# POOL waits for each two transfers by index to land before it issues the next two

## What is computed

```
x = ln(x + attention(x))          # 16 heads of 128, causal
x = ln(x + experts0(x))           # 32 experts 96 wide, top 6 by sigmoid, one shared expert of 192
x = ln(x + ssm(x))                # Mamba-2 style mixing: in_proj, conv of 4 taps, scan, gate, out_proj
x = ln(x + experts1(x))           # 16 experts 176 wide, in 4 groups, top 4, one shared expert of 352
```

## Time and profile before

| | us |
|---|---|
| median of 3 runs | 1851.53 |
| lowest, highest | 1841.31, 1858.38 |
| the profiled execution's own time | 1850.39 |
| its span, first to last instruction | 1848.6 |
| busy PE, DVE, ACT, POOL | 1493.5, 995.6, 751.7, 448.7 |
| DMA: moved by index, by SP's transfers | 41.96 MB, 288.31 MB |

### The profile page before, as it was taken

The page is one execution under the profiler, slowest core; times in us unless marked ns, Lnnn a source line. Parts: engine busy times, 40 slices in busy tenths (PEclk is TensorE's granted clock), DMA queues, the critical chain, the costliest instruction groups (busy, mean ns, idle before and its releaser), DMA issues.

```text
span 1848.6 us, 30360 instructions
## 1 busy us (share of the span) xinstructions
PE 1493.5 (81%) x9344; PEld 1240.5 (67%) x9344; DVE 995.6 (54%) x3299; ACT 751.7 (41%) x2326; POOL 448.7 (24%) x422
## 2 busy tenths in 40 slices
PE   7999999999997342688856888984689998798992
PEld 6988988988986342577745666773456667566661
DVE  5777777777777320161114757542486764154345
ACT  5555655655653100244423436430243633233420
POOL 1000000001000747100033420815342080222133
PEclk9999999999998655799987999995799999899996
DMA  8472461551600214089976755853155586799922
GB/s 301 159 263 68 193 254 39 229 219 50 253 1 1 94 56 156 29 276 313 315 250 185 237 167 162 266 156 122 53 180 180 166 260 193 240 297 309 321 90 74
DMA packets 173078, 331.71 MB, mean 179 GB/s; under 512 B 17280, under 2 KB 85888, under 8 KB 171680
## 3 DMA queue, kind: packets, MB, share of 16 engines
q1 hardware_dynamic: 157600, 288.31, 47.2%
q0 software_dynamic: 15360, 41.96, 6.8%
HBM read 196.41 MB, written 133.27 MB: 178 GB/s over the span
## 4 chain that ended last, share of the span: by engine, by line
PE 49%; DVE 17%; another core or an unknown queue 10%; issue 9%; ACT 7%; DMA 5%; POOL 2%; SPq 1%; DVEq 0%; ACTq 0%; POOLq 0%
PE psum L426 40%; DMA l_os<-b_out 4%; PE psum L1633 2%; DVE x L1142 2%; PE psum L1455 2%; ACT p_sb L766 1%; DVE s_sb L1171 1%; PE psum L1604 1%; PE psum L1466 1%; DVE conv L1256 1%; DVE stats L976 1%; DVE x L990 1%; ACT p_sb L764 1%; ACT kT_hi L742 1%
## 5 line engine op out<-in xcount | busy, mean ns | idle before, releaser
L426 PE MATMUL psum<-xbT,bw 128*96 128x128 f32 (+1 forms) x2392 | 325.7, 285 | 13.0 <-issue 6.8
L426 PEld LDWEIGHTS psum<-xbT,bw 128*96 128x96 f32 (+1 forms) x2392 | 298.5, 186 | 18.9 <-issue 11.2
L666 POOL DMA_INDIRECT og<-l_os,l_back_of x160 | 160.4, 1003 | 510.0 <-DMA l_os<-b_out 282.8
L426 PE MATMUL psum<-bw,b_act 96*128 96x256 f32 (+2 forms) x692 | 222.6, 413 | 72.3 <-ACT b_out L839 27.1
L1159 DVE TENSOR_TENSOR b_act<-psum,b_gated 96x128 f32<-96x128 f32 x190 | 53.9, 285 | 334.9 <-ACT b_gated L826 265.4
L650 POOL DMA_INDIRECT xs<-x,row_of x160 | 165.6, 1035 | 221.0 <-DVE row_of L1062 176.3
L426 PEld LDWEIGHTS psum<-bw,b_act 96*128 96x128 f32 (+2 forms) x692 | 107.8, 196 | 115.5 <-issue 74.8
L426 PE MATMUL psum<-l_shared_w,b_act 128*128 128x256 f32 (+1 forms) x192 | 71.4, 470 | 135.2 <-issue 71.6
L1154 DVE TENSOR_TENSOR b_act<-psum,b_gated 128x128 f32<-128x128 f32 x126 | 36.6, 290 | 254.4 <-ACT b_gated L823 198.2
L614 POOL TENSOR_TENSOR aw_lo<-aw_raw,aw_hi 128x512 fp32r<-128x512 f32 x32 | 41.2, 1291 | 484.7 <-ACT aw_hi L732 484.7
L839 ACT ACTIVATE b_out<-psum 128x256 f32<-128x256 f32 x252 | 96.7, 384 | 139.4 <-PE psum L426 83.8
(11 more groups left out here) (217 smaller groups left out, 3726.4 us busy)
## 6 DMA issues: line engine op xcount, KB each, us to landing
xs<-zeros SPq DMA_DIRECT2D x42, 1792.0 KB, 17.4
bw<-l_w SPq DMA_DIRECT2D x94, 640.0 KB
bw<-l_w SPq DMA_DIRECT2D x158, 320.0 KB
xb<-xs SPq DMA_DIRECT2D x252, 128.0 KB
l_os<-b_out SPq DMA_DIRECT2D x124, 256.0 KB
decay_all<-decay_dram SPq DMA_DIRECT2D x32, 384.0 KB
aw_raw<-attn_w SPq DMA_DIRECT2D x8, 1024.0 KB, 6.9
xs<-x,row_of POOLq DMA_INDIRECT x160
```

Of the source, the lines that this page charges most:

```text
L426: last = nc.tensor.matmul(out_ap, w, m, start=start and n == 0, stop=stop and n == len(pairs) - 1, **kw)
L666: pool.indirect_dma_start(og[:, i % MIX_RING, k, :], None, os[f["layer"]][t // HALF_TILES], bass.IndirectOffsetOnAxis(ap=back_of[f["layer" ...
```

## The change

A helper `transfer` issues every transfer by index. It keeps the semaphore values that the transfers issued since the last wait will bring. When two have been issued, it waits for both values before it issues a third; where both add to one semaphore, one wait on the later value stands for the two. The counts that a transfer's semaphore will have reached are worked out from what earlier transfers added to it (`earlier`), as constants. The order of all instructions, the transfers themselves and their semaphores stay as they are; nothing waits at the end of a run of transfers, only before the next transfer, so multiplications that follow a pair are not held up by it.

```diff
@@ -639,16 +639,31 @@
                 group(g)
             low_part(GROUPS - 1, 3)
 
+
+            latest = {}
+
+            def transfer(*args, done, value):
+
+                if latest.get("count") == 2:
+                    for semaphore, v in latest["values"]:
+                        pool.wait_ge(semaphore, v)
+                    latest.clear()
+                pool.indirect_dma_start(*args).then_inc(done, 16)
+                latest["values"] = [(s, v) for s, v in latest.get("values", ()) if s is not done] + [(done, value)]
+                latest["count"] = latest.get("count", 0) + 1
+
             def scatter(f, q, part=None):
 
                 if part in (None, 0):
                     if f["layer"] == 0 and q == 0:
                         pool.wait_ge(xs_zeroed, 16 * ZEROED * (GROUPS - 1))
                     pool.wait_ge(placed, QUADS * f["layer"] + q + 1)
+                earlier = f["layer"] * QUAD * L0["top"]
                 rows = [(t, k) for t in range(QUAD * q, QUAD * (q + 1)) for k in range(f["top"])]
-                for t, k in rows if part is None else rows[part:part + 1]:
-                    pool.indirect_dma_start(xs[q // 2], bass.IndirectOffsetOnAxis(ap=row_of[:, t, k:k + 1], axis=0), x[:, t, :], None) \
-                        .then_inc(scattered[q], 16)
+                for r, (t, k) in enumerate(rows):
+                    if part in (None, r):
+                        transfer(xs[q // 2], bass.IndirectOffsetOnAxis(ap=row_of[:, t, k:k + 1], axis=0), x[:, t, :], None,
+                                 done=scattered[q], value=16 * (earlier + r + 1))
 
             def all_stored(f, h):
 
@@ -662,9 +677,11 @@
                 i = f["layer"] * TILES + t
                 if ks[0] == 0:
                     wait(pool, combined, i - MIX_RING + 1)
+                earlier = sum(LAYERS[j // TILES]["top"] for j in range(i % MIX_RING, i, MIX_RING))
                 for k in ks:
-                    pool.indirect_dma_start(og[:, i % MIX_RING, k, :], None, os[f["layer"]][t // HALF_TILES],
-                                            bass.IndirectOffsetOnAxis(ap=back_of[f["layer"]][:, t, k:k + 1], axis=0)).then_inc(og_loaded[i % MIX_RING], 16)
+                    transfer(og[:, i % MIX_RING, k, :], None, os[f["layer"]][t // HALF_TILES],
+                             bass.IndirectOffsetOnAxis(ap=back_of[f["layer"]][:, t, k:k + 1], axis=0),
+                             done=og_loaded[i % MIX_RING], value=16 * (earlier + k + 1))
 
             def ssm_constants():
                 pool.wait_ge(o_added, LAST_OUT)
```

## The result

The changed kernel takes 1878.78 us (median of 4 runs, 1874.00 to 1889.06), the kernel before 1854.95 us beside it (4 runs, 1841.31 to 1871.95). The ratio is 1.0148, with a 95% interval of 1.0108 to 1.0189: slower by 1.5%, where the forecast said 1818 us and faster. The profiled execution of the changed kernel took 1877.07 us, its span is 1875.3 us.

A forecast was written before the change was run, and what follows sets the result against it. POOL's transfers, issued every 1.27 us but each occupying something shared for about 1.40, bound 603 to 754 us; elsewhere PE, except where POOL paces. -82 + 14 + 35 = -33 from 1850.4 gives 1818 us, eight-in-ten range 1765 to 1868.

The forecast's parts named there:

- Part (a): 603 to 787 us: stalls beside POOL's first scatter vanish, -94, less +12 drag by the pairs: -82 us.
- cover of 9 us: Near 700 us: scatter lets unit 32 start at 696, units arrive at 705; gone if a pair costs 0.4 us more.
- Part (b): 787 to 936 us: the other 24 scatter pairs now run beside the routed units on busy DMA: +14 us.
- Part (c): Stretches POOL paces, from 942 us to the end: waits cost more than cured stalls give back, together +35 us.
- gathers at 942: From 942.77 us: 24 gathers take 58 us instead of 46 and combining DVE waits for them: +8 us (0 to 12).
- run from 1237: From 1237 us: 14 pairs take 54 us against 35, but a 22 us stall goes: +4 us (-10 to 19).
- scatter at 1567: From 1567 us: 17 us of stalls go, but the scatter ends 9 us later: -9 us (-17 to 0).
- end: End of the kernel: eight gathers take 16.6 us against 8.9 + 2.9, all on the path: +5 us.
- The price of a pair: Time for two transfers with their wait: 3.6 us for quiet scatters, 4.2 for quiet gathers, 6.2 beside busy DMA.
- Stalls half cured: 603 to 776 us: signals are still held up, a unit takes 3.6 us, drag 50 instead of 12: 1856 us; 17%.
- waits turn out cheap: Whole kernel: quieter DMA makes all pairs cost 3.6 to 4.2 us and later costs mostly vanish: about 1758 us; 8%.
- Only waits: Mainly 603 to 776 us: stalls come from transfers' presence, not their rate, so pacing only adds waits: 1927 us; 14%.

The follow-up runs named there:

- free sittings: Sittings, each on one chip, in which the unchanged kernel before ran at 1705.56, 1708.08 and 1706.33 us.
- held: Sittings in which the unchanged kernel before ran at 1859.01 and 1855.64 us, as in the case itself (1854.95 us).
- experiment 85: Not a run's number: 85 us by experiment, between pairs in layer 0's scatters alone (1787.34 us) and pairs everywhere (1876.08 us), each against the kernel before.
- last sitting: Changed kernel rerun unedited beside the kernel before at its quicker level (1706.33 us): 1879.56 us, ratio 1.0998.
- the first and the third sitting: Two sets of follow-up runs with partial pacing or slower feeding; the unchanged kernel before took 1705.56 us in one, 1855.64 us in the other.
- Fours in the scatters: POOL waits after four transfers in the scatters of both layers, gathers unpaced, against the kernel before at 1855.64 us: 1781.03 us, ratio 0.9606.

## Why the prediction was wrong, point by point

**What bounds the kernel** was read rightly for the traced condition: the stalls from 603 to 754 us come with POOL's transfers, and slower feeding takes them away wholly or for the most part, in four different ways. That they might be a condition of the sitting and not of the kernel was nowhere considered; the runs shown (1841 to 1858) gave no hint of the level at 1706, and that profiled time and median agreed couldn't rule it out, since all were taken at one level. The 1.40 us a transfer is a figure of that level: in the free sittings the same feed of one in 1.27 us holds up nobody in 603 to 664 us. It is not the reason for the miss, as the case was measured held, but it is the reason why the gain there can't be counted on.

**Part (a), -82 forecast, -74.9 measured** at unit 32. Two errors met. Unit 10 came at 649 instead of 660: no drag by pairs (in the changed kernel PE is as busy from 603.70 to 664.50 as in the free kernel before, 49.13 and 49.07 us). But the cover of 9 us under the scatter's first half was not there. A pair in the quiet takes 3.93 us, not 3.6, since POOL goes on 1.70 us after its second issue has ended, and some are longer beside loads; the half's rows were complete near 704 instead of 690, and SP and PE waited (53.4 and 29.3 us). The forecast had named 0.4 us a pair as the point from which that cover is gone.

**Part (b), +14 forecast, +7.2 measured** (unit 32 to 111). With (a) that is -67.7, where the forecast had -68: partly luck, as (a) was 7 us off one way and (b) 7 the other. Pairs in layer 0's scatters alone gave -68.3 for the whole kernel.

**Part (c) is the step that failed: +35 forecast, +94.4 measured**, and by experiment 85 (from -68.3 with layer 0's scatters alone to +17.1 with all). Term by term, from the table above:

| stretch | forecast | measured |
|---|---|---|
| gathers at 942 (unit 111 to 123) | +8 | +15.2 |
| gathers at 1033, scatters at 1157 (to 172) | +9 +8 | +18.5 |
| run from 1237 (to 199) | +4 | +24.2 |
| gathers at 1357, scatters at 1481 (to 244) | +6 +8 | +14.0 |
| scatter at 1567 (to 252) | -9 | +6.5 |
| gathers at 1637 (to 299) | -4 | +6.8 |
| end | +5 | +9.2 |

The four mixed terms, transfers among multiplications, were right within 2 us. The largest miss is the run from 1237. The forecast priced the 28 transfers that ran there without a pause, 14 pairs. But behind them stood 24 more gathers of the same half, issued in two more runs after pauses of 13.24 and 6.21 us in which POOL waited for a combine. In the kernel before that was slack, and all 52 transfers took 84 us (1237.32 to 1321.80). With gathers at 4.1 to 4.8 us a pair the slack is used up, and the 52 become one chain of 114 us (1211.89 to 1326.07) on which DVE, and PE behind it, wait. At the forecast's own prices the 26 pairs would be 8 x 3.6 + 18 x 4.2 = 104 us, so 20 of the 30 us more come from the count of the transfers and 10 from the price. It is the same from 942 on, where the forecast priced 24 gathers and 36 became one chain of 89 us (875.53 to 964.60), and at the end: from 1790.36 to 1861.26 POOL issues 32 gathers in pairs, one chain again, where the forecast priced the last eight. The second miss is 1567: the forecast took off 17 us of stalls as a gain and counted 9 us for the later scatter, but its end stands before SP's load of the half's first rows (SP waits 21.6 us there, PE 16.9), and it was later by the growing delay of a pair beside loads, 5.3 to 6.4 us for the first three.

**The price of a pair** was the smaller error: 3.6 and 4.2 us in the quiet were taken for landing plus 0.3 us. Measured are 3.93 and 4.1 to 4.8. Beside loads the forecast had 6.2, and the second scatter's 24 pairs took 154.6 us, 6.4 each.

**The rivals.** "Stalls half cured" and "waits turn out cheap" are both out: nothing of the stalls is left in 603 to 754 us, and (c) cost more, not less. "Only waits" (1927 us) was right in its sign and wrong in its mechanism: it had the stalls stay. Yet its sentence from the Trainium skill ("DMA: Bandwidth & Descriptors", Rules for kernel authors: issue early, wait late) names what cost: by the last sitting, obeying it is worth 173 us where nothing stalls. The other sentence of the Trainium skill ("SBUF — State Buffer", SBUF: two separate sides), by which DMA and the compute engines cannot slow each other there, agrees with the free trace (PE busy 49.07 us beside 48 scatters), and the held one doesn't contradict it: there the engines' instructions are no longer, only further apart. That pacing would then cure nothing, as the prediction concluded, doesn't follow: the stalls have another cause and pacing cures them all the same.

**What stays open.** What puts a sitting at one level or the other was not found. It isn't the program, and it isn't a chip's number as recorded: the first and the third sitting bear the same one, free and held. Nor was it found what the transfers occupy. The packets of the transfers by index take 6.8% of 16 engines' 1848.6 us in the held trace of the kernel before, and 7.4% of 1708.5 us in its free one: 126 us in both, so it is not the moving of the data that is slower. One rival was not tested, the recording itself: the held trace of the kernel before holds 17700 records of semaphore updates, its free one 22820, and the changed kernel's have 20641 and 22855: records are missing at the held level, most of them in the kernel with the stalls. Whether the recording holds the engines, or both suffer from a third thing, isn't shown, and no execution here is known to have run without it. Missing records also mean that in held traces a part of the waits falls to "remote" or "issue".

**A version that loses at neither level.** Filling 256 columns before each of layer 0's scatters is faster by 3.8% held and the same (1.0005) free; it is the only one measured at both levels that never loses. Fours in the scatters are at 0.9606 held and weren't run free; pairs in layer 0's scatters win 3.6% held and lose 2.0% free.

## What to carry to other kernels

When a wait is added to a queue, don't price the transfers that ran without a pause; price the whole chain up to the last consumer, with every pause in it counted as slack that the new price uses up first. To limit what is under way, wait for the one before the last and not for all: the same limit of two cost 69 us instead of 173 in the free sittings; held it was not run. And before a stall is worth curing, look whether it is there in another sitting, since one trace and three runs at one time can't tell a kernel's property from a condition's.

## What the runs showed of the hardware

- The same kernel took 1701.05 to 1716.66 us in three sittings and 1841.31 to 1871.95 in three others, with nothing between. In the slower ones PE, ACT, DVE and SP get little done while POOL issues transfers by index without a pause: PE busy 12.36 us of 60.80 instead of 49.07, with their instructions as long as before (DVE busy 995.6 and 995.1 us in all). SP needs 12.60 us instead of 1.88 to issue four loads.
- The changed kernel, whose POOL lets each two transfers land, has the same time in both: 1878.78, 1876.08 and 1879.56 us.
- A pair of scatters, waited for in the quiet, takes 3.93 us, where two without a wait take 2.53; of gathers 4.1 to 4.8 us. With two always under way a scatter starts every 1.33 us at best, and every 1.51 us over the first 48 (pairs: 2.11).
- Waits after eight stall more than waits after four (unit 10 at 661.8 and 646.5 us), though less often waited for.
